# One stage of a four-layer network: the instruction orders of three engines laid out anew, other PSUM banks, three weight loads, factors in fours

## The chip, the cores and the metric

The program runs on one core of a Trainium2 chip. A core has TensorE (PE in the profile; its weight loads are PEld), VectorE (DVE), ScalarE (ACT), GpSimd (POOL) and SyncE (SP, which here only issues DMAs). Each engine works through its own list of instructions in order and waits at semaphores for the others. TensorE writes to PSUM, a memory of 8 banks of 2 KB per partition. The metric is the device time of one execution in microseconds (us).

## The reference

The network has four layers of cross-attention and feed-forward on x, (2, 1024, 256). The change touches the feed-forward of layer 1, whose two weights are reduced to three values times one scale (the code calls it the one-bit stage):

```python
def act_quant(x):
    scale = 127.0 / jnp.clip(jnp.max(jnp.abs(x), axis=-1, keepdims=True), 1e-05)
    return jnp.clip(jnp.round(x * scale), -128, 127) / scale

h = bit_linear(x, w1)                        # 256 -> 1024, on act_quant(x)
h = depthwise_conv1d(h.transpose(0, 2, 1), conv_w, conv_b)   # 3 taps along the tokens
h = jax.nn.silu(h.transpose(0, 2, 1))
return bit_linear(h, w2)                     # 1024 -> 256, on act_quant(h)
...
x = x + jnp.tanh(g_ffn[1]) * _L1_ffn_ref(_layernorm(x, axis=-1), L1_ffn_w1, ...)
# two steps later, the ternary layer, of whose weights the mean magnitude is needed first:
alpha = jnp.mean(jnp.abs(w))
w_t = jnp.sign(w) * (jnp.abs(w) > 0.5 * alpha)
```

## The kernel before

The 2048 tokens are 16 tiles of 128; tiles 0 to 7 are batch 0 (b = 0), 8 to 15 batch 1. x stays in SBUF as `K.x`. The stage is the class `BitFfn`, object `bit`; its steps are called one by one from hand-written lists, one per engine, at the end of `expert_choice_ffn`. Nothing else sets the order: an instruction starts when its engine has finished the one before and its semaphores are reached.

- Input side, in units u of two tiles: ScalarE `rows` normalises, VectorE `largest(g)` finds the row maxima of four tiles, ScalarE `quantise(g)` rounds, GpSimd `multiply_back(g)` scales back into `K.room`, TensorE `turn_rows(u)` transposes into bank 4+u (u below 4) or 6 or 7, ScalarE `high_part(u)` and VectorE `low_part(u)` split the value in two.
- Hidden side, n = 0 to 15 (eight blocks f of 128 hidden features for b = 0, then for b = 1): TensorE `up(n)`, 8 matmuls of 512 columns into the bank pair `PAIR[n]`; ScalarE `centre(n)`, the middle tap and bias; VectorE `taps(n)`, the two outer taps, two instructions over 1023 elements that read the same pair; ScalarE `silu(n)`. `centre(n)` also waits for `silu(n-2)`, and `up` into a used pair waits for the `taps` that read it.
- Output side, for the eight token tiles i of each batch: TensorE `turn(b, i)` transposes the tile's 1024 hidden values into the pair `TURN[b][i]`; VectorE `scale` takes the row maximum, clips, inverts, and multiplies out a fourth value that only `residual` needs; ScalarE `scaled` rounds; TensorE `turn_back` transposes into pair 0; ScalarE `copy_back`; TensorE `down` makes 256 columns in bank 6 or 7; VectorE `residual` adds them to x and takes the row statistics.
- Beside it stands work of the layers after: `TernaryWeights` (object `tw`) loads the two weights of layer 2 (1 MB each) over `K.room`, whose tiles `turn_rows` has read by then, both after `turn_rows(7)`; VectorE sums their magnitudes in eight `sum_piece` steps, adds them in `sum_end`, TensorE makes the total, VectorE makes `limits` and `signs`. `side.first_moments`, `first_rows`, `first_turns`, `first_copies` and `first_scores` begin the next attention. A barrier of all engines closes the stage.

`turn(0, 0)` waits for `silu(7)`, so from there TensorE mixes `up` of batch 1 with the three steps of the tokens of batch 0.

Of the kernel before, what the change touches and what calls it, by code (L numbers as in the profile page):

```python
# [1934 lines left out]
class BitFfn:  # L1935
# [245 lines left out]
    def scale(self, dve, b, i):  # L2181
        n, tv = b * TB + i, self.tv
        dve.wait_ge(self.t_ps, n + 1)
        t = Steps(self.t_step, 3 * n)
# [72 lines left out]
def expert_choice_ffn(nc, ctx, K, tag, ahead, buf, layer, acc_dram, nxt, make_bit, make_side, next_weights, old, cleared):  # L2257
# [12 lines left out]
    with ExitStack() as c:  # L2270
# [33 lines left out]
        with nc.Block(no_gpsimd_drain=True) as block:  # L2304
            @block.sync
            def _(sp):
# [1183 lines left out]
```

## Time and profile before

| | us |
|---|---|
| median of 3 runs (1058.43 to 1058.56) | 1058.54 |
| the profiled execution's own time | 1058.06 |
| its span (first to last instruction) | 1056.3 |
| busy over the span: PE, DVE, ACT, POOL | 968.4, 604.9, 488.6, 287.8 |

The stage lies at 461 to 572 us of the span. The page's shares are over the whole program, of which the stage is a tenth; for the stage the trace was asked for its own windows, waits and instructions in order of time. `PEclk` is the granted clock of TensorE as a share of full speed: 1.0 is 2.4 GHz and 0.5 is 1.2 GHz.

### The profile page before, as it was taken

The numbers are of one execution on the slowest core, as the hardware profiler recorded it, in microseconds if no ns is written. First come the engines' busy times: TensorE is split into PE (matmuls) and PEld (weight loads), VectorE is DVE, ScalarE is ACT, GpSimd is POOL, SyncE is SP. The second block draws the span as 40 slices with busy tenths as digits, with TensorE's granted clock in tenths as the row PEclk, the third lists the DMA queues.
The fourth block names the chain that finished last, engine by engine and source line by source line (L and its number), as shares of the span: only waits on it lengthen the run. The fifth ranks groups of instructions, "written<-read, shape, count | busy, mean of one in ns | idle before, by whom it ended". The sixth has DMA issues, their size and how long they took to land. (4 is left out here: it accounts for less than half of the span.)

```text
span 1056.3 us, 17895 instructions
## 1 busy us (share of the span) xinstructions
PE 968.4 (92%) x6340; PEld 831.4 (79%) x6341; DVE 604.9 (57%) x1265; ACT 488.6 (46%) x744; POOL 287.8 (27%) x271
## 2 busy tenths in 40 slices
PE   6999989989999999777788889999998899999997
PEld 5778868778888888455676768877786699999996
DVE  5858769942232213679798899767585622222221
ACT  3654422121111111687675587455552466656661
POOL 2000000033454532260005110610000244444442
PEclk9999999999999999988998699999999999999999
DMA  9200040035676654002000010070113322233332
GB/s 298 62 1 21 21 141 20 20 100 152 172 207 195 172 157 100 0 1 80 1 1 2 1 41 1 29 298 21 40 42 128 118 50 45 45 50 50 50 44 32
DMA packets 62483, 79.37 MB, mean 75 GB/s; under 512 B 7324, under 2 KB 46839, under 8 KB 62423
## 3 DMA queue, kind: packets, MB, share of 16 engines
q1 hardware_dynamic: 48791, 59.95, 16.9%
q0 software_dynamic: 13632, 18.62, 10.3%
q8 instruction: 37, 0.61, 0.2%
q14 instruction: 23, 0.19, 0.1%
HBM read 60.73 MB, written 17.83 MB: 74 GB/s over the span
## 5 line engine op out<-in xcount | busy, mean ns | idle before, releaser
L3123 PEld LDWEIGHTS ps<-room,xn_sb 128*128 128x128 f32 x1248 | 145.6, 192 | 2.7 <-issue 0.8
L3123 PE MATMUL ps<-room,xn_sb 128*128 128x128 f32 x1248 | 146.3, 275 | 0.6 <-issue 0.6
L282 POOL TENSOR_TENSOR norm_vec<-norm_vec,powers 128x4 f32<-128x4 f32 (+2 forms) x27 | 29.0, 1073 | 363.4 <-DVE norm_vec L276 363.4
L3076 POOL DMA_INDIRECT out_x<-f_yo,f_give x39 | 62.0, 1590 | 109.9 <-DVE f_yo L3321 94.4
L3192 ACT ACTIVATE xn_sb<-w_L_ffn_w 128x1024 f32 x78 | 82.2, 1057 | 20.8 <-DVE f_te L3289 10.8
L3315 DVE TENSOR_TENSOR room<-room,ps 128x512 f32<-128x512 f32 x39 | 26.8, 687 | 109.5 <-PE ps L3123 109.5
L2429 PE MATMUL ps<-b_room,room 128*128 128x256 f32 x384 | 85.6, 380 | 3.7 <-DVE room L2819 1.6
L2819 DVE TENSOR_TENSOR room<-room,ps 128x1024 f32<-128x1024 f32 x24 | 29.3, 1220 | 104.0 <-issue 89.5
L2429 PEld LDWEIGHTS ps<-b_room,room 128*128 128x128 f32 x384 | 72.6, 190 | 14.1 <-issue 1.8
L2386 POOL DMA_INDIRECT acc_rows<-f_eo,f_idx x32 | 52.4, 1637 | 94.6 <-DVE f_eo L2845 50.3
L2635 ACT ACTIVATE room<-ps 128x1024 f32<-128x1024 f32 x24 | 24.6, 1024 | 115.9 <-PE ps L2409 115.9
L492 PE MATMUL ps<-a_vblk,a_pT 128*128 128x51 f32 (+1 forms) x640 | 74.8, 272 | 0.0
L3131 PE MATMUL ps<-w_L_ffn_w,room 128*128 x312 | 73.9, 380 | 0.9 <-DVE room L3315 0.9
L492 PEld LDWEIGHTS ps<-a_vblk,a_pT 128*128 128x128 f32 (+1 forms) x640 | 74.0, 192 | 0.2 <-issue 0.2
L2409 PE MATMUL ps<-f_x_room,b_room 128*128 128x256 f32 x256 | 58.7, 382 | 3.6 <-ACT f_x_room L2665 3.6
L3131 PEld LDWEIGHTS ps<-w_L_ffn_w,room 128*128 128x128 f32 x312 | 56.2, 190 | 7.1 <-issue 1.1
L736 DVE TENSOR_REDUCE a_mx<-ps 128x16 f32<-128x1232 f32 x32 | 46.0, 1437 | 27.6 <-PE ps L466 14.2
L3197 ACT ACTIVATE room<-ps 128x512 f32<-128x512 f32 x39 | 23.3, 597 | 77.9 <-PE ps L3123 77.9
L2420 PE MATMUL ps<-f_x_room,b_room 128*128 128x256 f32 x256 | 57.9, 379 | 0.0
L2409 PEld LDWEIGHTS ps<-f_x_room,b_room 128*128 128x128 f32 x256 | 48.0, 190 | 11.7 <-issue 3.8
L481 PE MATMUL ps<-ident,a_pr 128*128 128x128 f32 x320 | 47.1, 278 | 7.3 <-ACT a_pT L684 2.5
L2420 PEld LDWEIGHTS ps<-f_x_room,b_room 128*128 128x128 f32 x256 | 48.6, 190 | 6.6
(402 smaller groups left out, 2059.5 us busy)
## 6 DMA issues: line engine op xcount, KB each, us to landing
w_L_ffn_w<-in_L_ffn_w SPq DMA_DIRECT2D x24, 512.0 KB, 8.7
b_room<-in_L_ffn_Wg SPq DMA_DIRECT2D x16, 512.0 KB, 4.8
b_room<-in_L_ffn_Wu SPq DMA_DIRECT2D x16, 512.0 KB, 5.8
b_room<-in_L_ffn_Wd SPq DMA_DIRECT2D x16, 512.0 KB, 6.4
xn_rows<-xn_sb SPq DMA_DIRECT2D x8, 512.0 KB, 2.9
x_sb<-in_x SPq DMA_DIRECT2D x4, 512.0 KB, 6.1
xn_sb<-in_L_ffn_w SPq DMA_DIRECT2D x2, 1024.0 KB, 7.6
x_sb<-acc_rows SPq DMA_DIRECT2D x4, 512.0 KB, 5.4
```

What stands on the lines that cost most here:

```text
L481: m = pe.transpose(ps[0:w, 4 + r % 2, (part - lo) * P:(part - lo + 1) * P], pr[:, n % 2, part * P:part * P + w], K.ident[:, :])
L492: m = pe.matmul(ps[:, 6, h * HV:(h + 3) * HV], pT[0:w, n % 2, part, :], vblk[0:w, n // TB, part, :, :].rearrange("p j c -> p (j c)"), star ...
L736: dve.tensor_reduce(mxt, sc, AX.X, ALU.max).then_inc(sh_step, 1)
L2386: pool.indirect_dma_start(acc_dram[:, :], bass.IndirectOffsetOnAxis(ap=idx[:, n:n + 1], axis=0), eo[e % 2][:, b, :], None, compute_op=ALU. ...
L2409: m = pe.matmul(ps[:, f // 2, (f % 2) * W:(f % 2 + 1) * W], g[:, k, f * P:(f + 1) * P], rhs[k], start=(k == 0), stop=(k == KT - 1))
L2420: m = pe.matmul(ps[:, 2 + f // 2, (f % 2) * W:(f % 2 + 1) * W], u[:, k, f * P:(f + 1) * P], rhs[k], start=(k == 0), stop=(k == KT - 1))
L2429: m = pe.matmul(ps[:, 4 + p, j * D:(j + 1) * D], hT[p][:, f, j * P:(j + 1) * P], w[:, f, :], start=(f == 0), stop=(f == FT - 1))
L2819: dve.tensor_tensor(hT[p][:, :, :].rearrange("p a c -> p (a c)"), ge[p][:, :], ps[:, 2:4, :].rearrange("p a c -> p (a c)"), ALU.mult).then ...
L3076: pool.indirect_dma_start(out_rows[:, :], bass.IndirectOffsetOnAxis(ap=give[:, j:j + 1], axis=0), yo[j % 2][:, :], None, compute_op=ALU.ad ...
L3123: m = pe.matmul(ps[:, banks[p], f * P:(f + 1) * P], wb[p][:, n, i, f * P:(f + 1) * P], xsT[p][:, i * P:(i + 1) * P], start=(i == 0), stop= ...
L3131: m = pe.matmul(ps[:, Y_BANK, 0:D], hid[p][:, f * P:(f + 1) * P], w2[:, e, f, :], start=(f == 0), stop=(f == FT - 1))
L3192: act.activation(wb[p][:, n, :, :], w[:, e, :, :], ACT.Copy).then_inc(w_sb, 1)
```

## The change

It does five things, all in this stage.

1. The load of the next weights is cut in three: the first weight in two halves of 512 KB, issued after `turn_rows(1)` and `turn_rows(3)` (each half overwrites four tiles of `K.room`), the second weight after `turn_rows(7)` as before.
2. `sum_piece` waits for the half that it reads, with two more semaphores. Its four calls for the first weight stand ahead of `taps(0)` on VectorE.
3. `scale` no longer makes the fourth value; `out_factors(g)` makes it for four tiles at once, and `residual` waits for that.
4. Other bank pairs: pair 3 (banks 6 and 7) is used by `up(8)`, `up(11)` and `up(14)`, and `turn(0, 0)` and `turn(0, 7)` go to pair 2.
5. The three hand-written lists are in another order.

```diff
-    def sync(self, sp):
-        for dst, src in self.loads:
-            sp.dma_start(dst, src).then_inc(self.loaded, 16)
+    def load_up(self, sp, half):
+        dst, src = self.loads[0]
+        sp.dma_start(dst[:, half, :], src[:, half, :]).then_inc((self.half0, self.half1)[half], 16)
+
+    def load_down(self, sp):
+        dst, src = self.loads[1]
+        sp.dma_start(dst, src).then_inc(self.loaded, 16)
...
-        dve.wait_ge(self.loaded, 32)
+        dve.wait_ge((self.half0, self.half1)[q // 2] if n == 0 else self.loaded, 16)
...
-    PAIR = (0, 1, 2, 0, 1, 2, 0, 1, 2, 0, 2, 2, 2, 2, 2, 2)
-    TURN = ((1, 1, 1, 1, 1, 1, 1, 1), (1, 2, 1, 2, 1, 2, 1, 2))
+    PAIR = (0, 1, 2, 0, 1, 2, 0, 1, 3, 0, 2, 3, 2, 2, 3, 1)
+    TURN = ((2, 1, 1, 1, 1, 1, 1, 2), (1, 2, 1, 2, 1, 2, 1, 2))
...
         dve.reciprocal(tv[:, 2, n:n + 1], tv[:, 1, n:n + 1]).then_inc(self.sc_ready, 1)
-        t.did(dve.tensor_scalar(tv[:, 3, n:n + 1], tv[:, 1, n:n + 1], self.wv[:, 3, 1:2], None, ALU.mult))
+
+    def out_factors(self, dve, g):
+        n, tv = 4 * g, self.tv
+        dve.wait_ge(self.t_step, 2 * n + 8)
+        dve.tensor_scalar(tv[:, 3, n:n + 4], tv[:, 1, n:n + 4], self.wv[:, 3, 1:2], None, ALU.mult).then_inc(self.factor, 1)
...
+                sp.wait_ge(bit.x_ps, 2)
+                next_weights.load_up(sp, 0)
+                sp.wait_ge(bit.x_ps, 4)
+                next_weights.load_up(sp, 1)
                 sp.wait_ge(bit.x_ps, TB)
-                next_weights.sync(sp)
+                next_weights.load_down(sp)
...
+                bit.turn(pe, 0, 0)
+                bit.turn(pe, 0, 1, (bit.y_sb, 8))
+                bit.up(pe, 10, (bit.qf_sb, 1))
...
+                bit.up(pe, 14, (bit.x_done, 4))
+                bit.up(pe, 15, (bit.qf_sb, 7))
...
+                side.first_copies(act)
                 bit.copy_back(act, 1, 7)
-                side.first_copies(act)
```

VectorE, the start of the stage. Before (`low_part` 0 to 3, `taps(0)`, `largest(3)`; `f_va` is the buffer of the convolution):

```order
L2105 TENSOR_TENSOR f_xl_1<-ps,f_xh_1 128x2x256 [waits f3_xh_sb] x4
L2140 SCALAR_TENSOR_TENSOR f_va<-ps,f_cws,f_va 128x1023 [waits f3_y0]
L2143 SCALAR_TENSOR_TENSOR f_va<-ps,f_cws,f_va 128x1023 [waits f3_tap]
L2065 TENSOR_REDUCE f_vec<-xn_sb 128x4 [waits f3_n_by_act]
L2067 TENSOR_SCALAR f_vec<-f_vec 128x4 [waits f3_amax]
L2069 RECIPROCAL f_vec<-f_vec 128x4 [waits f3_amax]
```

Now (L974 is `sum_piece`; the two semaphores of the halves bear older names here):

```order
L2109 TENSOR_TENSOR f_xl_1<-ps,f_xh_1 128x2x256 [waits f3_xh_sb] x4
L2069 TENSOR_REDUCE f_vec<-xn_sb 128x4 [waits f3_n_by_act]
L2071 TENSOR_SCALAR f_vec<-f_vec 128x4 [waits f3_amax]
L2073 RECIPROCAL f_vec<-f_vec 128x4 [waits f3_amax]
L974 TENSOR_REDUCE tw_part<-room 128x8 [waits a0_vblk] x2
L974 TENSOR_REDUCE tw_part<-room 128x8 [waits a0_bvb] x2
L2144 SCALAR_TENSOR_TENSOR f_va<-ps,f_cws,f_va 128x1023 [waits f3_y0]
L2147 SCALAR_TENSOR_TENSOR f_va<-ps,f_cws,f_va 128x1023 [waits f3_tap]
L2109 TENSOR_TENSOR f_xl_1<-ps,f_xh_1 128x2x256 [waits f3_xh_sb] x2
```

`largest(3)` and four `sum_piece` came ahead of `taps(0)`, and `low_part` 4 and 5 directly behind it.

VectorE where the tokens of batch 0 begin, after `taps(8)`. Before (`scale(0, 0)` in four instructions, then `taps(9)`):

```order
L2185 TENSOR_REDUCE f_tv<-ps 128x1 [waits f3_t_ps]
L2187 TENSOR_SCALAR f_tv<-f_tv 128x1 [waits f3_t_step]
L2189 RECIPROCAL f_tv<-f_tv 128x1 [waits f3_t_step]
L2190 TENSOR_SCALAR f_tv<-f_tv,f_wv 128x1
L2140 SCALAR_TENSOR_TENSOR f_va<-ps,f_cws,f_va 128x1023 [waits f3_y0]
L2143 SCALAR_TENSOR_TENSOR f_va<-ps,f_cws,f_va 128x1023 [waits f3_tap]
```

Now:

```order
L2189 TENSOR_REDUCE f_tv<-ps 128x1 [waits f3_t_ps]
L2191 TENSOR_SCALAR f_tv<-f_tv 128x1 [waits f3_t_step]
L2193 RECIPROCAL f_tv<-f_tv 128x1 [waits f3_t_step]
L2189 TENSOR_REDUCE f_tv<-ps 128x1 [waits f3_t_ps]
L2191 TENSOR_SCALAR f_tv<-f_tv 128x1 [waits f3_t_step]
L2193 RECIPROCAL f_tv<-f_tv 128x1 [waits f3_t_step]
L974 TENSOR_REDUCE tw_part<-room 128x8 [waits a0_kt]
L2144 SCALAR_TENSOR_TENSOR f_va<-ps,f_cws,f_va 128x1023 [waits f3_y0]
L2147 SCALAR_TENSOR_TENSOR f_va<-ps,f_cws,f_va 128x1023 [waits f3_tap]
```

Two tokens' `scale` of three instructions each and the first piece of the second weight now stand ahead of `taps(9)`.

ScalarE at the same place. Before (`centre(10)`, `scaled(0, 0)`, `copy_back(0, 0)`, `silu(9)`, `centre(11)`, `scaled(0, 1)`):

```order
L2133 ACTIVATE f_va<-ps,w_L_ffn_conv_b,f_cws 128x1024 [waits f3_a_sb,f3_h_ps]
L2197 ACTIVATE xn_sb<-ps,f_magic,f_tv 128x1024 [waits f3_sc]
L2205 ACTIVATE f_qT<-ps,f_magic 128x1024 [waits f3_u_ps]
L2148 ACTIVATE xnT_sb<-f_va 128x1024 [waits f3_y_sb]
L2133 ACTIVATE f_va<-ps,w_L_ffn_conv_b,f_cws 128x1024 [waits f3_a_sb,f3_h_ps]
L2197 ACTIVATE xn_sb<-ps,f_magic,f_tv 128x1024 [waits f3_sc]
```

Now (`silu(8)`, `scaled(0, 0)` and `(0, 1)`, `centre(10)`, `silu(9)`, `copy_back(0, 0)`, `centre(11)`):

```order
L2152 ACTIVATE xnT_sb<-f_va 128x1024 [waits f3_y_sb]
L2205 ACTIVATE xn_sb<-ps,f_magic,f_tv 128x1024 [waits f3_sc] x2
L2137 ACTIVATE f_va<-ps,w_L_ffn_conv_b,f_cws 128x1024 [waits f3_a_sb,f3_h_ps]
L2152 ACTIVATE xnT_sb<-f_va 128x1024 [waits f3_y_sb]
L2213 ACTIVATE f_qT<-ps,f_magic 128x1024 [waits f3_u_ps]
L2137 ACTIVATE f_va<-ps,w_L_ffn_conv_b,f_cws 128x1024 [waits f3_a_sb,f3_h_ps]
```

`scaled` of both first tokens went ahead of `centre(10)`, and `copy_back(0, 0)` behind `silu(9)`.

## Rows read from the trace of the kernel before

**Rows 1.** Windows of the stage and the stretch after; busy us (instructions) per engine.
```profile
core 0: us, PE busy (x) PEld busy (x) DVE busy (x) ACT busy (x) POOL busy (x), PEclk, DMA share, GB/s
462.45:500.00 37.55, 29.07 (x111) 21.86 (x109) 30.51 (x32) 30.04 (x34) 7.34 (x7) 0.85 0.16 56
500.00:548.00 48.00, 38.52 (x264) 31.29 (x264) 41.29 (x76) 32.27 (x31) 0.00 (x0) 0.96 0.00 1
572.00:593.00 21.00, 18.31 (x73) 15.66 (x73) 14.18 (x49) 10.80 (x21) 8.35 (x6) 0.52 0.00 1
```

**Rows 2.** Waits from 462.45 to 570.45; total us, times, longest.
```profile
DVE f_va L2140 <- ACT f_va L2133: 11.6, 7, 4.0
DVE f_tv L2185 <- PE ps L2158: 0.5, 2, 0.2
ACT f_va L2133 <- PE ps L2124: 10.8, 7, 2.9
ACT xn_sb L2197 <- DVE f_tv L2189: 6.4, 7, 1.9
```

**Rows 3.** VectorE in order of time (start us, duration us): first and last steps.
```profile
459.97 2.48 DVE L2105 TENSOR_TENSOR f_xl<-ps,f_xh 128x512 fp32r<-128x512 f32 x4
466.43 1.28 DVE L2140 SCALAR_TENSOR_TENSOR f_va<-ps,f_cws,f_va 128x1023 f32<-128x1023 f32 x1 [3.98 <-ACT f_va L2133]
...
570.02 0.43 DVE L2220 BATCH_NORM_STATS2 bn_st<-x_sb 128x6 f32<-128x256 f32 x1
```

**Rows 4.** VectorE in order of time: the spacing of its steps.
```profile
495.77 1.23 DVE L2185 TENSOR_REDUCE f_tv<-ps 128x1 f32<-128x1024 f32 x1 [0.24 <-PE ps L2158]
...
497.30 0.19 DVE L2190 TENSOR_SCALAR f_tv<-f_tv,f_wv 128x1 f32<-128x1 f32 x1
497.41 1.27 DVE L2140 SCALAR_TENSOR_TENSOR f_va<-ps,f_cws,f_va 128x1023 f32<-128x1023 f32 x1
...
499.92 1.27 DVE L2140 SCALAR_TENSOR_TENSOR f_va<-ps,f_cws,f_va 128x1023 f32<-128x1023 f32 x1
...
530.10 0.68 DVE L970 TENSOR_REDUCE tw_part<-room 128x8 f32<-128x512 f32 x1
530.70 0.47 DVE L2217 SCALAR_TENSOR_TENSOR x_sb<-ps,f_tv,x_sb 128x256 f32<-128x256 f32 x1
```

**Rows 5.** ScalarE in order of time, before and after `centre(0)`.
```profile
462.02 2.06 ACT L307 ACTIVATE xn_sb<-x_sb,norm_vec  x4
...
468.02 1.21 ACT L2133 ACTIVATE f_va<-ps,w_L_ffn_conv_b,f_cws 128x1024 f32<-128x1024 f32 x1 [1.62 <-PE ps L2124]
469.24 1.28 ACT L2148 ACT_TABLE_LOAD   x1
470.53 1.06 ACT L2148 ACTIVATE b_room<-f_va 128x1024 f32<-128x1024 f32 x1
```

**Rows 6.** TensorE in order of time: `up`, transposes, and idle time before them.
```profile
461.40 0.77 PE L2124 MATMUL ps<-f_xh,f_q 128*128 128x512 f32 x1 [2.33 <-DVE f_xl L2105]
...
464.95 0.63 PE L2124 MATMUL ps<-f_xh,f_q 128*128 128x512 f32 x1
...
477.82 0.79 PE L2124 MATMUL ps<-f_xh,f_q 128*128 128x512 f32 x1 [2.60 <-DVE f_va L2143]
...
500.15 1.07 PE L2167 MATMUL ps<-ident,xn_sb 128*128 128x128 f32 x8 [2.45 <-ACT xn_sb L2197]
501.05 1.66 PE L2158 MATMUL ps<-ident,b_room 128*128 128x128 f32 x8
...
516.08 0.50 PE L2124 MATMUL ps<-f_xh,f_q 128*128 128x512 f32 x1 [1.59 <-DVE f_va L2143]
...
517.81 0.39 PE L2124 MATMUL ps<-f_xl,f_q 128*128 128x512 f32 x1
...
569.30 1.91 PE L938 MATMUL ps<-keys_a,xnT_sb 128*128 128x77 f32 x16
```

**Rows 7.** DMA issues in the stage: KB each, us to landing.
```profile
room<-in_L_ffn_w_up SPq DMA_DIRECT2D x1, 1024.0 KB, 4.9
```

**Rows 8.** GpSimd in order of time: the next attention's rows.
```profile
554.06 9.86 POOL L906 TENSOR_SCALAR xn_sb<-x_sb,norm_vec 128x256 f32<-128x256 f32 x8
```

More of the change, by code:

```diff
@@ L2556, in _ @@
                 bit.up(pe, 1, (nxt.s_x, 8))
-                bit.turn_rows(pe, 4, (bit.xl_sb, 3))
-                bit.turn_rows(pe, 5, (bit.xl_sb, 4))
+                bit.turn_rows(pe, 4)
+                bit.turn_rows(pe, 5)
                 bit.up(pe, 2)
+                bit.turn_rows(pe, 6, (bit.xl_sb, 5))
                 bit.up(pe, 3, (bit.y_sb, 1))
@@ L2562, in _ @@
                 bit.up(pe, 5, (bit.y_sb, 3))
+                bit.turn_rows(pe, 7, (bit.xl_sb, 6))
                 bit.up(pe, 6, (bit.y_sb, 4))
-                bit.turn_rows(pe, 6, (bit.xl_sb, 5))
-                bit.turn_rows(pe, 7, (bit.xl_sb, 6))
                 bit.up(pe, 7, (bit.y_sb, 5))
-                bit.up(pe, 8, (bit.y_sb, 6))
+                bit.up(pe, 8, (bit.xl_sb, 8))
                 bit.up(pe, 9, (bit.y_sb, 7))
-                bit.turn(pe, 0, 0, (bit.y_sb, 8))
-                bit.up(pe, 10, (bit.y_sb, 9))
+                bit.turn(pe, 0, 0)
@@ L2571, in _ @@
+                bit.turn(pe, 0, 1, (bit.y_sb, 8))
+                bit.up(pe, 10, (bit.qf_sb, 1))
+                bit.up(pe, 11, (bit.y_sb, 9))
                 bit.turn_back(pe, 0, 0, (bit.y_sb, 10))
-                bit.turn(pe, 0, 1, (bit.qf_sb, 1))
-                bit.up(pe, 11, (bit.y_sb, 11))
-                bit.down(pe, 0, 0, (bit.xl_sb, 7))
                 bit.turn(pe, 0, 2, (bit.qf_sb, 2))
                 bit.turn_back(pe, 0, 1, (bit.u_sb, 1))
-                bit.up(pe, 12, (bit.y_sb, 12))
@@ L2578, in _ @@
-                bit.down(pe, 0, 1, (bit.xl_sb, 8))
+                bit.up(pe, 12, (bit.y_sb, 11))
                 bit.turn(pe, 0, 3, (bit.qf_sb, 3))
                 bit.turn_back(pe, 0, 2, (bit.u_sb, 2))
+                bit.down(pe, 0, 0, (bit.y_sb, 12))
+                bit.down(pe, 0, 1)
+                bit.turn(pe, 0, 4, (bit.qf_sb, 4))
                 bit.up(pe, 13, (bit.y_sb, 13))
                 bit.turn_back(pe, 0, 3, (bit.u_sb, 3))
+                bit.turn(pe, 0, 5, (bit.qf_sb, 5))
@@ L2591, in _ @@
+                bit.up(pe, 15, (bit.qf_sb, 7))
                 bit.turn_back(pe, 0, 5, (bit.u_sb, 5))
-                bit.down(pe, 0, 4, (bit.x_done, 3))
-                bit.turn(pe, 0, 7, (bit.qf_sb, 7))
+                bit.down(pe, 0, 4, (bit.y_sb, 15))
+                bit.turn(pe, 0, 7)
                 bit.turn_back(pe, 0, 6, (bit.u_sb, 6))
-                bit.down(pe, 0, 5, (bit.x_done, 4))
+                bit.turn(pe, 1, 0, (bit.y_sb, 16))
+                bit.down(pe, 0, 5)
+                bit.turn(pe, 1, 1, (bit.qf_sb, 8))
@@ L2596, in _ @@
+                bit.turn_back(pe, 0, 7, (bit.u_sb, 7))
                 bit.down(pe, 0, 6, (bit.x_done, 5))
-                bit.turn_back(pe, 0, 7, (bit.u_sb, 7))
-                bit.turn(pe, 1, 0, (bit.qf_sb, 8))
+                bit.turn(pe, 1, 2, (bit.qf_sb, 9))
                 bit.down(pe, 0, 7, (bit.x_done, 6))
-                bit.turn(pe, 1, 1, (bit.y_sb, 16))
-                bit.turn_back(pe, 1, 0, (bit.u_sb, 8))
-                bit.turn(pe, 1, 2, (bit.qf_sb, 9))
-                bit.down(pe, 1, 0, (bit.x_done, 7))
+                bit.turn_back(pe, 1, 0)
@@ L2720, in _ @@
                 bit.silu(act, 5)
-                bit.high_part(act, 7)
                 bit.centre(act, 7)
@@ L2925, in _ @@
                 bit.low_part(dve, 3)
+                bit.largest(dve, 3)
+                bit.tw.sum_piece(dve, 0, 0)
+                bit.tw.sum_piece(dve, 0, 1)
+                bit.tw.sum_piece(dve, 0, 2)
+                bit.tw.sum_piece(dve, 0, 3)
                 bit.taps(dve, 0)
-                bit.largest(dve, 3)
+                bit.low_part(dve, 4)
+                bit.low_part(dve, 5)
                 bit.taps(dve, 1)
```

122 lines of the change are left out of this document (59 added, 63 removed).

## The prediction

> **What bounds the stage now.** I read the windows first, then the waits, then VectorE and TensorE in order of time. The page's totals (TensorE 92% busy) are a mean over the whole program and say nothing here. In the windows [rows 1] VectorE is the fullest engine of the stage: 30.51 of 37.55 us and 41.29 of 48.00, against TensorE's 29.07 and 38.52, part of which ran below full clock (0.85 and 0.96). The waits [rows 2] show where VectorE's idle time comes from: 11.6 us in 7 waits of `taps` for `centre`, 0.5 us for a transpose. `centre` in turn waited 10.8 us for `up`, and `scaled` 6.4 us for `scale`. So this is a ring of three engines in which none is full, and what ends last is the order in which they serve each other. The longest wait is the first, 3.98 us ahead of `taps(0)` [rows 3].
>
> VectorE's own account: from the end of `low_part(3)` (459.97 + 2.48 = 462.45) to its last instruction (570.02 + 0.43 = 570.45) are 108.0 us [rows 3]. Idle are 11.6 + 0.5 = 12.1 [rows 2], so the work with its gaps is 95.9. TensorE ends 0.8 us later, at 569.30 + 1.91 = 571.2 [rows 6], and the barrier follows. The stage can gain at most the 12.1 us of idle and what is taken off the work.
>
> **The edits with a price of their own.**
> - Factors in fours. The fourth instruction of `scale` takes 497.41 - 497.30 = 0.11 us of VectorE [rows 4]. Sixteen go, four of 128x4 come: 12 x 0.11 = 1.3 us less. The new wait of `residual` is for an instruction that stands ahead of it on the same engine; its bound is one fresh wait of 0.1 us per group, so between 0.9 and 1.3. I take 1.3.
> - Three loads. SP waits for `turn_rows(1)` and `(3)` with nothing else queued behind but the second weight. The fourth `turn_rows` is over before the 461.40 of `up(0)` [rows 6]; a load of 1024 KB landed in 4.9 us [rows 7], so the second half, 512 KB, is there by 466.3 at the latest. Its readers come after 467 (below). Price 0; if a load were later than that, every us would count, since VectorE would stand before `taps(0)`.
> - Banks. No instruction is added. The new pairs only lift or add waits, which the walk below contains.
>
> **The new order, walked through.** I take the three new lists, the semaphores in the code, and spacings of the trace: `scale` 1.64 less 0.11 = 1.53, `taps` 499.92 - 497.41 = 2.51, `sum_piece` 0.60 [rows 4], four rows of ScalarE 2.06, `centre` 1.2 [rows 5], `up` (464.95 - 461.40) 3.5 us at half clock and (517.81 - 516.08) x 8/7 = 2.0 at full, eight transposes 1.0 [rows 6].
> - Start. ScalarE ends `rows(3)` at 462.02 + 2.06 = 464.1 [rows 5]. VectorE idles until then (1.65 us), does `largest(3)` to 465.7 and four `sum_piece` (2.4 us) to 468.1. ScalarE quantises to 467.8 and ends `centre(0)` at 469.0. So `taps(0)` starts at 469.0, which is 2.6 later than before, but `largest(3)` and half of the sums are behind it. Idle here: 1.65 + 0.9, instead of 3.98.
> - `taps(0)` to `taps(8)`. Each `up` comes out at least 1.5 us ahead of its `centre`, and each `centre` just as VectorE is free. The `low_part` steps that before stood between fall in the same gaps. I get `taps(8)` at 491.6 and no wait over 0.1.
> - Tokens of batch 0. With `turn(0, 0)` in pair 2 and `turn(0, 1)` in pair 1, two `scale` stand together (494.1 to 497.2) while ScalarE rounds the first. `up(10)` waits for that rounding, until 497.0; `taps(10)` then starts at 500.3, `taps(12)` at 509.2, where VectorE has waited 0.6 for `turn(0, 3)`. From there `scale`, `residual` and the pieces of the second weight fill the pauses; `taps(15)` starts at 527.0, the last `residual` of batch 0 ends at 538.0, with about 0.5 us of further waits.
> - Batch 1. `first_moments` comes near 544 instead of 551, so that GpSimd's eight rows, 9.86 us [rows 8], end some 3 us before the stage does. VectorE has 22 us of work left and TensorE 17.6 (20 groups of eight at 0.88) plus `first_scores`; I find no wait over 0.2. `down(1, 7)` now waits for a `copy_back` behind `first_copies` and starts at 557.8, and `first_scores` ends at 560.7.
>
> New account of VectorE: work 95.9 - 1.3 = 94.6, idle 1.65 + 0.9 + 1.1 = 3.65, end at 462.45 + 98.25 = 560.7, 9.8 us earlier. TensorE's end moves from 571.2 to 560.7, 10.5. I take 10.0.
>
> **What I take off.** The walk is full of ties (a result that arrives within 0.2 us of its use); I allow 0.5 us. The clock: TensorE fell to 1.2 GHz with idle stretches of 2.60 and 2.45 us, and not with 1.59 [rows 6]. The walk has one pause of 2.3 us (before `up(10)`), and several of 1.5 to 1.8. One fall costs an `up` 1.5 us. I charge two thirds of one, 1.0. The gain is 10.0 - 0.5 - 1.0 = 8.5.
>
> The silu table load took 1.28 us and the `silu` began 0.01 us behind it [rows 5]. The Trainium skill, "ScalarE: Activation LUTs", What ACT_TABLE_LOAD costs, adds a drain and gives about 2.66 us for the pair; by that the second `centre` after it would be 1.4 us later and, after the 0.6 us of slack that the walk has there, the gain 0.7 us smaller. The trace differs, and I go by it.
>
> **Rivals.**
> - A, small gain. The ties fail: each of the about 30 handoffs from `scale` to `scaled` to `turn_back` to `copy_back` runs late by 0.1 to 0.15 us, since the spacings were measured with other neighbours. Half of the 8.5 us that idle time gave (12.1 - 3.65) comes back: gain 4.3 + 1.3 less 1.0 for the clock = 4.6, time 1053.5. For it: 6.4 us of such waits before [rows 2]. Against: VectorE's durations hardly vary. Chance 0.18.
> - B, the clock in the next stage. After the barrier TensorE ran at 0.52 for 21 us, with 18.31 us busy [rows 1]. Its tail before the barrier is denser now than it was. If it starts that stretch at full clock, its 18.3 busy us shrink to about 10, of which perhaps half is on the path: 4 to 5 us more, time 1045. Against: the pause of the barrier itself stays. Chance 0.12.
> - C, no change. The halves land late or a wait that I overlooked holds `taps(0)` and one later chain; this needs a stall of 8 us or a lasting spread of small ones. Nothing in the rows has it. 1056.5 to 1060.5, chance 0.04.
> - D, slower. TensorE in batch 0's tokens, 493 to 538, at 1.2 GHz. There it has 6 `up` and 27 groups of eight: at full 6 x 1.9 + 27 x 0.88 = 35 of 45 us; at half, with about 1.5 per group (one took 1.66 with its tail [rows 6]) and 3.5 per `up`, 61.5. With a share h at half it needs 35 + 26.5h. It delays anything from h = 0.38, and eats the whole 10 us from h = 0.76; all of it at half gives 16 us, less 10 gained: 1064. For it: many pauses between small groups. Against: 0.96 over 500 to 548 [rows 1], or h = 0.08, with longer pauses. Chance 0.04. This is what the Trainium skill, "TensorE: Matmul & The Clock Gate", A second HAM failure mode: psum-queue depth-cycling, warns of (short idle times between groups that cycle through banks make the clock swing); by that rule the time would lie between A and D. The trace agrees only for the early stretch, 0.85 before 500 us [rows 1], where `up` has slack.
>
> **How the numbers follow.** Against its own time: 1058.06 - 8.5 = 1049.6; the median of the runs is 0.5 above the profiled execution, so I give 1049.8. The forecast's own range is 1047.5 to 1052.5, chance 0.62; below it lies B, above it A, then C and D. For 8 in 10 I take half of B and most of A: 1045.8 to 1054.5. Under 0.2% (2.1 us) a change of this kernel can't be told from none. Faster 0.92 (forecast, A, B), same 0.04, slower 0.04.
>
> **What would show it.** In the trace after: `taps(0)` starts near 469.0 with four `sum_piece` ahead of it and no wait for a load; the waits of `taps` for `centre` shrink from 11.6 to below 3 us; two `scale` stand together before `taps(9)`; VectorE is over 95% busy from 469 to its end, which comes near 561 to 562; the stage after starts 8 to 10 us earlier and takes as long as before. I am wrong on A if those waits stay above 5 us, on D if the granted clock from 493 to 538 is under 0.8, and on the load if VectorE waits for SP before `taps(0)`. The stages before 455 should not move at all.

## The result and the profile after

| | before | after |
|---|---|---|
| median of the runs, us | 1058.55 (1058.43 to 1058.80, 4 runs) | 1050.82 (1049.33 to 1051.95, 4 runs) |
| ratio, 95% interval | | 0.9933 [0.9909, 0.9957] |
| the profiled execution's own time, us | 1058.06 | 1049.91 |
| its span, us | 1056.3 | 1048.2 |

The change makes the kernel 7.7 us faster (0.7%). 1049.8 was forecast, with 1045.8 to 1054.5 as the range. The changed kernel's line numbers are 4 to 8 higher than those of before (`taps` L2144, `scale` L2189, `up` L2128).

First the windows of the changed kernel, the same two stretches as in [rows 1], and the 20 us that follow its barrier.

```profile
core 0: us, PE busy (x) PEld busy (x) DVE busy (x) ACT busy (x) POOL busy (x), PEclk, DMA share, GB/s
462.45:500.00 37.55, 28.56 (x119) 21.40 (x119) 34.64 (x38) 30.47 (x34) 6.74 (x6) 0.91 0.09 28
500.00:548.00 48.00, 42.34 (x320) 36.24 (x319) 44.25 (x83) 38.11 (x36) 1.67 (x2) 0.99 0.00 1
563.90:583.90 20.00, 17.21 (x72) 14.87 (x72) 14.04 (x48) 10.58 (x21) 8.35 (x6) 0.57 0.00 1
```

In the first stretch VectorE is busy 34.64 us instead of 30.51, in the second 44.25 instead of 41.29. Then VectorE's waits over the stage, to be laid beside [rows 2].

```profile
DVE f_va L2144 <- ACT f_va L2137: 2.0, 2, 1.1
DVE f_vec L2069 <- ACT xn_sb L307: 1.7, 1, 1.7
DVE f_tv L2189 <- PE ps L2162: 1.1, 2, 0.8
```

The seven waits of `taps` for `centre`, 11.6 us, have become two of 2.0 us together. New is one of `largest(3)` for the rows that ScalarE still makes. Where they stand is seen in VectorE's instructions in order of time (start, duration, in brackets the idle time before it and what ended it); they answer to [rows 3].

```profile
459.37 2.48 DVE L2109 TENSOR_TENSOR f_xl<-ps,f_xh 128x512 fp32r<-128x512 f32 x4
463.51 1.22 DVE L2069 TENSOR_REDUCE f_vec<-xn_sb 128x4 f32<-128x1024 f32 x1 [1.67 <-ACT xn_sb L307]
...
465.06 2.43 DVE L974 TENSOR_REDUCE tw_part<-room 128x8 f32<-128x512 f32 x4
468.39 1.28 DVE L2144 SCALAR_TENSOR_TENSOR f_va<-ps,f_cws,f_va 128x1023 f32<-128x1023 f32 x1 [0.89 <-ACT f_va L2137]
...
490.88 1.28 DVE L2144 SCALAR_TENSOR_TENSOR f_va<-ps,f_cws,f_va 128x1023 f32<-128x1023 f32 x1
...
500.71 1.28 DVE L2144 SCALAR_TENSOR_TENSOR f_va<-ps,f_cws,f_va 128x1023 f32<-128x1023 f32 x1 [1.11 <-ACT f_va L2137]
...
561.13 0.43 DVE L2228 BATCH_NORM_STATS2 bn_st<-x_sb 128x6 f32<-128x256 f32 x1
```

The first row starts 0.6 us earlier than before. That isn't the change: in the second trace of the same kernel (after again, below) it starts at 459.97, as before. So I measure the stage from here on by itself: from the start of `low_part(0)` (this first row) to TensorE's first instruction behind the barrier. That was 572.82 - 459.97 = 112.85 us before and is 563.89 - 459.37 = 104.52 now: the stage gained 8.3 us. TensorE around `up(10)` and at the barrier, in order of time:

```profile
496.29 0.50 PE L2128 MATMUL ps<-f_xh,f_q 128*128 128x512 f32 x1 [2.21 <-ACT xn_sb L2205]
...
497.10 0.63 PE L2128 MATMUL ps<-f_xl,f_q 128*128 128x512 f32 x1
497.52 0.63 PE L2128 MATMUL ps<-f_xh,f_q 128*128 128x512 f32 x1
...
560.03 1.91 PE L938 MATMUL ps<-keys_a,xnT_sb 128*128 128x77 f32 x16
563.89 0.63 PE L1061 MATMUL ps<-ident,xn_sb 128*128 128x128 f32 x4 [1.96 <-PEq L100]
```

The clock did fall at `up(10)`: its matmuls follow each other every 0.42 us, where they take 0.23 at full clock.

### The profile page after: what moved, and what is told of

It is laid out like the page before. It is cut to its first block and busy times, and to the rows that moved or that the text cites. A ratio compares the mean times of both kernels' runs of the same rounds, so it can differ in the third digit from the quotient of the medians.

```text
span 1048.2 us, 17878 instructions
## 1 busy us (share of the span) xinstructions
PE 964.9 (92%) x6340; PEld 829.7 (79%) x6341; DVE 603.3 (58%) x1253; ACT 489.6 (47%) x744; POOL 288.2 (27%) x271
## 5 line engine op out<-in xcount | busy, mean ns | idle before, releaser
L2398 POOL DMA_INDIRECT acc_rows<-f_eo,f_idx x32 | 52.4, 1638 | 94.6 <-DVE f_eo L2857 49.6
```

The costliest lines, as they stand in the source:

```text
L2398: pool.indirect_dma_start(acc_dram[:, :], bass.IndirectOffsetOnAxis(ap=idx[:, n:n + 1], axis=0), eo[e % 2][:, b, :], None, compute_op=ALU. ...
```

## Experiments

"After" is the changed kernel. Each ratio is to runs of the kernel before on the same chip. Most executions of one kernel lie within 4 to 5 us of each other, single ones further off (of 59 executions of the kernel before that ran beside these experiments 56 took 1055.1 to 1059.7 us, and one 1064.0). So the stage's length in the trace, as defined above, is the finer measure, but each length is from one trace.

| kernel | ratio, 95% interval | stage, us | against `after` |
|---|---|---|---|
| before | | 112.85 | +8.3 |
| after | 0.9933 [0.9909, 0.9957] | 104.52 | |
| after again | 0.9932 [0.9914, 0.9950] | 104.53 | 0.0 |
| fours_only (on before) | 1.0010 [0.9997, 1.0023] | 112.76 | -0.1 against before |
| sums_only (on before) | 1.0004 [0.9981, 1.0026] | 112.90 | 0.0 against before |
| start_new_tokens_old | 1.0000 [0.9986, 1.0014] | 111.34 | -1.5 against before |
| fours_undone | 0.9938 [0.9918, 0.9958] | 104.59 | +0.1 |
| sums_late | 0.9969 [0.9953, 0.9984] | 108.10 | +3.6 |
| banks_old | 1.0136 [1.0118, 1.0155] | 126.50 | +22.0 |
| ups_old | 1.0104 [1.0081, 1.0128] | 118.04 | +13.5 |
| fill | 0.9916 [0.9898, 0.9935] | 102.92 | -1.6 |
| start | 0.9932 [0.9907, 0.9957] | 102.14 | -2.4 |
| best | 0.9906 [0.9891, 0.9921] | 101.99 | -2.5 |
| best_hold | 0.9901 [0.9870, 0.9931] | 102.02 | -2.5 |

**after again**, the changed kernel once more, without an edit.

> The changed kernel itself, once more, for its spread: its four runs so far lie in two pairs, 1049.3 and 1049.9, and 1051.7 and 1052.0, while the kernel before keeps within 0.4 us. Theory: the stage ends at the same time in each (first TensorE row after the barrier at 563.9, within 0.4), and the 2 us come later, from how long TensorE stays at 1.2 GHz in the stages after. Rival: they come from inside the stage, from the fall of the clock at up(10); then VectorE's wait for centre(10) varies between 0 and 1.2 us and the barrier with it. Time 1049.3 to 1052 in both.

The stage took 104.53 us, the kernel 1049.11 (1048.05 to 1051.55). In these two traces the stage repeats to 0.01 us, and what differs lies behind it (2.5 us, the last section) and ahead of it (0.6 us). It isn't always as close. Where the lists are the same up to `taps(8)`, that step starts 31.5 us behind the start of the stage in five traces (after, after again, fours_undone, banks_old and fill) and 32.4 in ups_old, whose granted clock was 0.50 from 472.8 to 479.6, where theirs was 1.00. I read differences of the stage below 1 us as open, unless VectorE's rows explain them.

**sums_late**, the four sums of the first weight back among the tokens:

```diff
-                bit.tw.sum_piece(dve, 0, 0)   # and 1, 2, 3, ahead of taps(0)
...
                 bit.out_factors(dve, 0)
+                bit.tw.sum_piece(dve, 0, 0)
+                bit.tw.sum_piece(dve, 0, 1)
...
                 bit.scale(dve, 0, 5)
+                bit.tw.sum_piece(dve, 0, 2)
...
+                bit.tw.sum_piece(dve, 0, 3)
                 bit.scale(dve, 0, 6)
```

> The changed kernel with the four magnitude sums of the first weight put back among the tokens of batch 0 (two behind scale(0, 3), one each behind scale(0, 5) and ahead of scale(0, 6)); loads, banks, factors and all other orders stay. Theory (VectorE's work after taps(0) sets the end): taps(0) still starts at 468.4, since ScalarE's quantise(3) stands ahead of centre(0), with 3.3 us of idle ahead of it instead of 0.9, and the 2.4 us of sums are paid later: 1050.8 + 2.4 = 1053.2, less at most 0.5 that fits into waits. Rival (the ring of handoffs sets the end, VectorE has room): the sums fall into pauses and the time stays within 0.7 of 1050.8.

The stage is 3.6 us longer. VectorE and TensorE in order of time:

```profile
469.24 1.28 DVE L2144 SCALAR_TENSOR_TENSOR f_va<-ps,f_cws,f_va 128x1023 f32<-128x1023 f32 x1 [3.24 <-ACT f_va L2137]
...
520.30 1.23 DVE L2189 TENSOR_REDUCE f_tv<-ps 128x1 f32<-128x1024 f32 x1 [1.73 <-PE ps L2162]
```
```profile
514.81 0.50 PE L2128 MATMUL ps<-f_xh,f_q 128*128 128x512 f32 x1 [1.23 <-DVE f_va L2147]
...
515.88 0.63 PE L2128 MATMUL ps<-f_xl,f_q 128*128 128x512 f32 x1
```

The wait ahead of `taps(0)` is 3.24 us instead of 0.89: the 2.35 us that the sums had filled are idle again, as the theory had it. The rest goes with another fall of the clock, at `up(12)`, after a pause of only 1.23 us, and 1.73 us of wait behind it.

**fours_only and sums_only**, one part each on the kernel before: the factors in fours, and the two half loads with the four sums ahead of `taps(0)`.

```diff
-        t.did(dve.tensor_scalar(tv[:, 3, n:n + 1], tv[:, 1, n:n + 1], self.wv[:, 3, 1:2], None, ALU.mult))
+    def out_factors(self, dve, g): ...        # fours_only, behind scale(b, 3) and scale(b, 7)
```
```diff
+                bit.tw.sum_piece(dve, 0, 0)   # sums_only; also 1, 2, 3; none of them later
                 bit.taps(dve, 0)
```

> The kernel before with the out factors made four at a time (12 instructions of VectorE fewer, 1.3 us of its work), nothing else changed. Theory (before the change the ring of three engines sets the pace in batch 0 and VectorE's work only in batch 1): about half of it counts, 0.5 to 0.9 us faster: 1057.7 to 1058.0. Rival (VectorE's work counts all through): 1.3 us, 1057.2. Rival (nothing): 1058.5.

> The kernel before with the loads in three pieces and the four magnitude sums of the first weight ahead of taps(0), where VectorE idled 3.98 us; all else as before. Theory: the 2.4 us of sums cost nothing in the new place; in the old places about half of them lay in VectorE's pauses in batch 0, so 1 to 1.8 us are gained: 1056.7 to 1057.5. Rival (all counts): 2.4 us, 1056.1. Rival (the old pauses hid them): within 0.4 us of before.

Neither moves the stage (112.76 and 112.90), so in both the rival holds by which nothing is gained. In sums_only the wait of `taps(0)` shrinks from 3.98 to 1.61 us, but VectorE's waits for `centre` sum to nearly what they were (11.6 before):

```profile
DVE f_va L2144 <- ACT f_va L2137: 11.1, 7, 2.5
```

In fours_only they sum to 10.6, and those for a transpose to 1.9 instead of 0.5. In the old order VectorE's work isn't what sets the end; time taken off it comes back as waiting.

**start_new_tokens_old**, the kernel before with the new loads and the new lists up to `taps(8)`, and the old lists and banks from there:

```diff
                 bit.taps(dve, 8)              # up to here as in the changed kernel
                 bit.scale(dve, 0, 0)          # from here as before
                 bit.taps(dve, 9)
```

> Half of the change: loads in three, and the new orders of all three engines up to taps(8), up(7) and silu(8); from scale(0, 0), up(8) and centre(10) on the old orders and old banks, and the factors one by one. Theory (VectorE's account): at taps(8) it is 1.3 us earlier than before, as the changed kernel is (491.5 against 492.9 with equal starts), and the 2.4 us of sums are behind it; then the old ring with its waits of about 8 us takes over and swallows part of the 2.4: gain 2 to 3.7 us, 1054.9 to 1056.5. The other 4 to 6 us belong to the token part. Rival (the gain is made at the start): 6 us or more are gained here.

The stage is 1.5 us shorter, of 8.3, and less than the 2 to 3.7 expected; the ratio of whole kernels, 1.0000 with an interval of 0.14% to either side, can't tell it from nothing. Of its waits for `centre` 7.7 us in 5 are left, three of them (2.20, 2.26 and 1.41 us) at `taps(11)` to `taps(13)`. Most of the gain is in the token part, where the new lists and the new banks come together.

**fours_undone**, the changed kernel with the fourth instruction back in each `scale`:

```diff
+        t.did(dve.tensor_scalar(tv[:, 3, n:n + 1], tv[:, 1, n:n + 1], self.wv[:, 3, 1:2], None, ALU.mult))
-                bit.out_factors(dve, 0)       # and 1, 2, 3
```

> The changed kernel with the factors made one by one as before; all else stays. Theory (VectorE is now the bound from taps(0) to the end): all 12 extra instructions count, 1.2 us slower than the changed kernel, 1052.0 against 1050.8. Rival (they fit in waits): within 0.5 us of it.

The stage is 0.1 us longer, and VectorE's last instruction 0.25 us later (102.00 instead of 101.75 us from the start). Two pieces of VectorE's time order, first after again, then fours_undone, tell why:

```profile
546.57 0.17 DVE L276 TENSOR_SCALAR norm_vec<-norm_vec 128x8 f32<-128x8 f32 x1
546.65 0.22 DVE L2198 TENSOR_SCALAR f_tv<-f_tv,f_wv 128x4 f32<-128x4 f32 x1
546.98 0.48 DVE L2225 SCALAR_TENSOR_TENSOR x_sb<-ps,f_tv,x_sb 128x256 f32<-128x256 f32 x1
```
```profile
546.23 0.20 DVE L2194 TENSOR_SCALAR f_tv<-f_tv,f_wv 128x1 f32<-128x1 f32 x1
546.35 0.17 DVE L267 TENSOR_TENSOR norm_vec<-bn_st 128x8 f32<-128x8 f32 x1
```

A fourth instruction costs 0.12 us to the next start. `out_factors` costs 0.33 where `residual` waits for it at once (two of the four stand so) and 0.12 to 0.15 elsewhere. From `scale(1, 1)` to the end of VectorE that is 7 x 0.12 - 0.33 - 0.15 = 0.36 us saved, and the traces differ by 0.34 there; the like saving ahead of it is hidden, since the waits for `centre` and `turn` are 3.1 us with the fours and 2.7 without. The rival (they fit in waits) holds.

**banks_old**, the three new orders with the old bank pairs and the waits that they need:

```diff
-    PAIR = (0, 1, 2, 0, 1, 2, 0, 1, 3, 0, 2, 3, 2, 2, 3, 1)
-    TURN = ((2, 1, 1, 1, 1, 1, 1, 2), (1, 2, 1, 2, 1, 2, 1, 2))
+    PAIR = (0, 1, 2, 0, 1, 2, 0, 1, 2, 0, 2, 2, 2, 2, 2, 2)
+    TURN = ((1, 1, 1, 1, 1, 1, 1, 1), (1, 2, 1, 2, 1, 2, 1, 2))
...
-                bit.turn(pe, 0, 1, (bit.y_sb, 8))
-                bit.up(pe, 10, (bit.qf_sb, 1))
-                bit.up(pe, 11, (bit.y_sb, 9))
+                bit.turn(pe, 0, 1, (bit.qf_sb, 1))
+                bit.up(pe, 10, (bit.y_sb, 9))
+                bit.up(pe, 11, (bit.y_sb, 11))
```

> The changed kernel with the bank pairs of the kernel before (up(8) in pair 2, up(11) and up(14) in pair 2, up(15) in pair 2, turn(0, 0) and turn(0, 7) in pair 1) and the waits that go with them; the three orders stay new. Theory (orders and banks belong together): turn(0, 1) now waits for the rounding of the first token, so scale(0, 1), which stands ahead of taps(9), comes about 3 us later, and up(11) to up(15) each wait for the taps that read pair 2, so that taps(11) waits about 3 us for centre(11) and taps(14), taps(15) 2 to 3 us each: the stage is 6 to 12 us longer than the 104.5 of the changed kernel, that is as long as before (112.9) or longer. Rival (the orders carry the gain, banks only remove small waits): stage 105 to 107.5.

The stage takes 126.5 us, 13.7 more than before, beyond both expectations. VectorE's long waits in it:

```profile
499.25 1.23 DVE L2189 TENSOR_REDUCE f_tv<-ps 128x1 f32<-128x1024 f32 x1 [3.29 <-PE ps L2162]
513.03 1.23 DVE L2189 TENSOR_REDUCE f_tv<-ps 128x1 f32<-128x1024 f32 x1 [6.56 <-PE ps L2162]
520.23 1.23 DVE L2189 TENSOR_REDUCE f_tv<-ps 128x1 f32<-128x1024 f32 x1 [3.09 <-PE ps L2162]
541.67 1.28 DVE L2144 SCALAR_TENSOR_TENSOR f_va<-ps,f_cws,f_va 128x1023 f32<-128x1023 f32 x1 [5.11 <-ACT f_va L2137]
549.38 1.28 DVE L2144 SCALAR_TENSOR_TENSOR f_va<-ps,f_cws,f_va 128x1023 f32<-128x1023 f32 x1 [4.52 <-ACT f_va L2137]
```

They sum to 22.6 us, about the whole loss of 22.0. The granted clock from 500 to 548 us is 0.78 in this kernel. The new orders without the new banks are far worse than the old orders. The opposite kernel, the old orders with the new banks, was not run; what the banks are worth by themselves is not shown.

**ups_old**, only `up(11)` and `up(14)` back in pair 2:

```diff
-    PAIR = (0, 1, 2, 0, 1, 2, 0, 1, 3, 0, 2, 3, 2, 2, 3, 1)
+    PAIR = (0, 1, 2, 0, 1, 2, 0, 1, 3, 0, 2, 2, 2, 2, 2, 1)
...
-                bit.up(pe, 11, (bit.y_sb, 9))
+                bit.up(pe, 11, (bit.y_sb, 11))
-                bit.up(pe, 14, (bit.x_done, 4))
+                bit.up(pe, 14, (bit.y_sb, 14))
```

> The changed kernel with up(11) and up(14) alone back in pair 2, where they wait for the taps of the block before that read the same pair; turn(0, 0), turn(0, 7) and up(8) keep their new pairs. With all banks old the stage took 126.5 us, 22 more than the 104.5 of the changed kernel, and VectorE's long waits were 3.3 us ahead of scale(0, 1), 6.6 and 3.1 ahead of scale(0, 2) and (0, 3), 5.1 and 4.5 ahead of taps(14) and (15). Theory (what counts is that up(11) and up(14) can run ahead of the taps of up(10) and up(13)): four of those five waits come back, and the stage is 12 to 18 us longer than 104.5. Rival (the first token's pair is what sets the rest going, the ups only follow): the waits ahead of scale(0, 2) and (0, 3) shrink below 3 us in sum and the stage is 4 to 8 us longer.

The stage is 13.5 us longer than in the changed kernel, in the theory's range. 0.9 of them stand ahead of `taps(8)`, where nothing was edited (see after again), so about 12.6 belong to the two pairs. Three waits return, not four (VectorE, and then the `up(11)` that causes the first one, on TensorE):

```profile
511.11 1.22 DVE L2189 TENSOR_REDUCE f_tv<-ps 128x1 f32<-128x1024 f32 x1 [6.67 <-PE ps L2162]
518.31 1.22 DVE L2189 TENSOR_REDUCE f_tv<-ps 128x1 f32<-128x1024 f32 x1 [3.09 <-PE ps L2162]
539.42 1.28 DVE L2144 SCALAR_TENSOR_TENSOR f_va<-ps,f_cws,f_va 128x1023 f32<-128x1023 f32 x1 [4.78 <-ACT f_va L2137]
```
```profile
504.49 0.80 PE L2128 MATMUL ps<-f_xh,f_q 128*128 128x512 f32 x1 [3.93 <-DVE f_va L2147]
```

`turn(0, 2)` stands behind `up(11)` on TensorE, so when `up(11)` waits 3.93 us for `taps(10)` to free its pair, and then runs at half clock, the next `scale` waits too. The price holds the falls of the clock that the new waits bring with them; the trace doesn't separate the two.

**fill**, 16 transposes of the identity into banks that nothing reads, ahead of `up(10)`:

```diff
                 bit.turn(pe, 0, 1, (bit.y_sb, 8))
+                pe.wait_ge(bit.y_sb, 9)
+                bit.keep_busy(pe, 16)
                 bit.up(pe, 10, (bit.qf_sb, 1))
```

> The changed kernel with 16 transposes of the identity (into banks 6 and 7, which nobody reads then) between turn(0, 1) and up(10), where TensorE idled 2.21 us and then ran at 1.2 GHz for 3.4 us. They end before the wait of up(10) does. Theory (the fall of the clock costs what VectorE then waits): up(10) takes 1.9 instead of 3.2 us, VectorE's wait of 1.11 us for centre(10) goes to below 0.2, and 0.8 to 1.3 us of the time go, if the next wait, for turn(0, 3), does not take them. Rival (the ring has slack behind up(10)): within 0.3 us of the changed kernel.

**start**, `centre(0)` ahead of `quantise(3)` on ScalarE, two sums ahead of `largest(3)` on VectorE:

```diff
-                bit.quantise(act, 3)
                 bit.centre(act, 0)
+                bit.quantise(act, 3)
...
-                bit.largest(dve, 3)
                 bit.tw.sum_piece(dve, 0, 0)
                 bit.tw.sum_piece(dve, 0, 1)
+                bit.largest(dve, 3)
```

> The changed kernel with centre(0) ahead of quantise(3) on ScalarE (it idled 1.71 us there, waiting for largest(3)) and two of the four sums ahead of largest(3) on VectorE (it idled 1.67 us there). Theory (all of VectorE's idle ahead of taps(0) is on the path): taps(0) starts at 466.3 to 466.6 instead of 468.4, and about 2 us of the time go. Rival (quantise(3), pushed by centre(0), delays turn_rows(6) and with it up(3), or centre(1) comes late): taps(0) is early and taps(1) or taps(2) wait for it; under 0.7 us are gained.

The five us after the start of `up(10)`, windows of after, of fill and of start:

```profile
496.29:501.29 5.00, 5.00 (x15) 3.97 (x16) 3.82 (x6) 3.02 (x3) 0.00 (x0) 0.66 0.01 3
```
```profile
496.95:501.95 5.00, 5.00 (x28) 4.29 (x29) 4.81 (x7) 3.62 (x4) 0.00 (x0) 1.00 0.00 0
```
```profile
496.66:501.66 5.00, 5.00 (x28) 4.30 (x29) 4.82 (x7) 3.62 (x4) 0.00 (x0) 1.00 0.00 0
```

In fill the pause before `up(10)` is 0.47 us, the clock stays at 2.4 GHz, `taps(10)` doesn't wait, and the stage is 1.6 us shorter, the price of that fall and more than the 0.8 to 1.3 expected. That the transposes are what kept the clock up isn't shown by this one trace. In start the clock stays up as well, though nothing was done for it and the pause is as long as in after:

```profile
496.66 0.50 PE L2128 MATMUL ps<-f_xh,f_q 128*128 128x512 f32 x1 [2.22 <-ACT xn_sb L2205]
```

So of its 2.4 us 1.6 are the fall that didn't happen, and about 0.8 the order: `taps(8)` starts 30.7 us behind `low_part(0)` instead of 31.5. `taps(0)` even starts at 6.9 instead of 9.0, as expected, but of these 2.1 us 1.07 are waited for again at `taps(2)`. The whole kernel, 1048.48 us with a ratio of 0.9932, can't be told from the changed one.

**best**, start and fill together.

> The changed kernel with both improvements that the earlier runs pointed to: centre(0) ahead of quantise(3) on ScalarE and two sums ahead of largest(3) on VectorE, and 16 transposes of the identity on TensorE ahead of up(10), so that the clock doesn't fall there. Alone they shortened the stage by 2.4 and 1.6 us (104.5 to 102.1 and to 102.9). If they are independent the stage takes 100.5 to 101.0 us and the kernel 1046.5 to 1047.5 where the kernel before takes 1056.5. Rival: in the better start up(10) no longer has a pause long enough for the clock to fall, so the transposes have nothing to save, and the stage stays at 102.0 to 102.3.

The stage took 101.99 us, the kernel 1048.10 (1045.36 to 1048.65): the rival's number, and not by its reason. The rival said that the pause would be too short; it was there in start, 2.22 us. What was missing was the fall, and so the transposes had nothing to save. It beats the kernel before by 0.94%, and in the stage the changed kernel by 2.5 us; the two ratios (0.9906 and 0.9933) have intervals that overlap.

**best_hold**, best with 12 more transposes in the stage behind the barrier, for rival B:

```diff
                 turn_a(2)
+                for j in range(12):
+                    pe.transpose(ps[:, 5, (j % 4) * P:(j % 4 + 1) * P], K.ident[:, :], K.ident[:, :])
                 turn_p(0)
```

> As best, and in the stage after the barrier 12 more transposes of the identity into a bank that is free there, between the first four transposes and those that wait 1.42 us for ScalarE's softmax. Question: whether that stretch, which ran 20 us at 1.2 GHz in all kernels so far, is held at 2.4 GHz when the second of its two pauses (1.95 us at the barrier, 1.42 us right behind) is filled. If it is: TensorE's busy 17 to 18 us of the 20 shrink by half, and the kernel is 3 to 5 us faster than best (rival B of the prediction). If the pause of the barrier alone makes the clock fall: nothing, or up to 1 us slower, since the 12 transposes take 1.3 us at full and 2.6 at half clock.

The first 20 us behind the barrier, best and then best_hold; and TensorE in order of time in best_hold:

```profile
561.83:581.83 20.00, 17.37 (x72) 15.01 (x72) 14.04 (x48) 10.54 (x21) 8.31 (x6) 0.57 0.01 1
```
```profile
562.55:582.55 20.00, 15.39 (x95) 13.40 (x96) 16.67 (x55) 12.55 (x23) 8.34 (x6) 0.91 0.01 1
```
```profile
565.95 1.99 PE L1105 MATMUL ps<-ctx_nat,f_pT 77*128 77x256 f32 x8 [0.25 <-ACT f_pT L1264]
570.17 2.82 PE L938 MATMUL ps<-keys_a,xnT_sb 128*128 128x77 f32 x16 [2.23 <-ACT xnT_sb L1253]
```

The clock was held, 0.91 instead of 0.57; in the 13 other traces the same 20 us stand at 0.50 to 0.57, so here the transposes are the cause. From the barrier to the first row of the stage after that one are 106.92 us instead of 109.51: 2.6 us. TensorE then waits 2.23 us for ScalarE; the stretch was bound by more than TensorE. The kernel as a whole took 1048.23 us (1043.26 to 1053.51), the same as best, where 3 to 5 us less were expected: in the profiled execution the program behind that point took 377.5 us instead of 372.3. In it the clock fell for 3.4 us behind that point and again 24 us later, and for 10.2 us at 800 us, where best has one stretch of 3.4. Whether the transposes bring this about, or it is the spread of the last section, one trace doesn't tell.

## Why the prediction was right, and where its terms were off

The walk, counted from the start of `low_part(0)` (459.97 in the prediction, 459.37 in after):

| step | predicted | measured |
|---|---|---|
| `taps(0)` starts | 9.0 | 9.0 |
| `taps(8)` starts | 31.6 | 31.5 |
| `up(10)` starts, pause | 37.0, 2.3 | 36.9, 2.2 |
| `taps(10)` starts | 40.3 | 41.3 |
| wait of `scale(0, 3)` | 0.6 | 0.8 |
| `taps(15)` starts | 67.0 | 68.7 |
| last `residual` of batch 0 ends | 78.0 | 79.9 |
| `first_moments` | 84.0 | 85.8 |
| VectorE ends | 100.7 | 102.2 |
| gain of the stage | 10.0 - 1.5 = 8.5 | 8.3 |

- **What bounds the stage.** Right: the order in which the engines serve each other. VectorE's idle time for `centre` went from 11.6 to 2.0 us. It is 94.4% busy from `taps(0)` to its end (87.97 of 93.17 us); over 95% was forecast.
- **Where the gain comes from.** Right as a whole, and the experiments add what the walk couldn't show: fours, sums and the new start bring nothing, nothing and 1.5 us in the old token part, and the orders without the banks lose 13.7 us against before. The prediction had given the banks no price of their own and left them to the walk. They are the largest condition of the change that was measured: `up(11)` and `up(14)` in pair 3 alone are worth about 12.6 us in this order. How the remaining 6.8 us of gain split between the lists of the three engines is open; none of the lists was put back alone in the token part.
- **VectorE's account.** From the end of `low_part(3)` (461.85) to its end (561.56) are 99.7 us, 4.7 of them idle and 95.0 work. The walk had 3.65 and 94.6, and 1.5 us were allowed for ties and the clock. So the account missed 1.1 us of idle and 0.4 of work, 1.5 in all. That the two match to 0.1 us is in part luck, since the clock was priced too low and the ties and the fours too high.
- **Factors in fours, 1.3 us.** Wrong in size: 0.1 us of the stage, 0.25 of VectorE's end. The 0.11 us that I had taken for the new instruction is 0.33 where its reader stands right behind it (1.0 us of work saved instead of 1.3 in all), and most of that fell into waits, which grew by 0.4 us. The lower bound of 0.9 left out that the saving could be hidden.
- **Loads at price 0.** Right. The halves were issued at 454.8 and 458.5 and landed in 3.2 us (median), and the sums began at 465.06 without a wait for them. Moving the sums early was worth 3.6 us in the new order, of which 2.35 are the filled wait.
- **The clock, 1.0 us.** The place was right, the price 1.6 (two thirds of 1.5 had been charged), and the reason was wrong. I had read from [rows 6] that pauses of 2.45 us and more make the clock fall and 1.59 doesn't. It fell behind 1.23 us in sums_late and stayed behind 2.22 in start. Behind longer pauses it stayed too: 2.82 us in banks_old and 2.93 in ups_old, with 1.00 in the five us that follow each. The 2.2 us pause of the walk was therefore neither safe nor sure to cost, and that two thirds of a fall were near the measured price is luck.
- **Ties, 0.5 us.** From `taps(10)` on the measured steps lie 1.0 to 1.9 us behind the walk, and 1.5 at the end. The fall explains 1.0 at `taps(10)` and 1.6 of the stage by fill, so about nothing is left for the ties. The gain of the stage, 8.5 by the sum and 8.3 measured, is right by 0.2 us with fours and ties too large and the clock too small.
- **The table load.** As before, `silu(0)` begins 0.01 us behind the load:

```profile
470.43 1.28 ACT L2152 ACT_TABLE_LOAD   x1
471.72 1.06 ACT L2152 ACTIVATE b_room<-f_va 128x1024 f32<-128x1024 f32 x1
```

  The 2.66 us of the Trainium skill, "ScalarE: Activation LUTs", What ACT_TABLE_LOAD costs, don't appear between the `centre` before, which ends at 470.41, and the `silu`. (The prediction's sum by that page, 1.4 less 0.6 us of slack, is 0.8 and not the 0.7 that it gives.)
- **From 8.5 us to 1049.8.** The prediction adds 0.5 us to 1049.6 and writes 1049.8; by its own terms it is 1050.1, which lies nearer to the measured 1050.8.
- **Rival A (small gain)** fails by its own mark: 2.0 us of waits for `centre`, where it needed more than 5. **Rival D (slower)** too: the granted clock from 493 to 538 us is 0.96. Its mechanism exists, though: in banks_old the clock is 0.78 over 500 to 548 us and the kernel 1.4% slower than before. **Rival B (the clock in the next stage)** didn't come by itself, 0.57 instead of 0.50 in the 20 us behind the barrier. Forced in best_hold it gave 2.6 us, less than the 4 to 5 of the prediction; TensorE's 2.23 us of wait for ScalarE there show that it no longer sets the path alone.
- **From 8.3 to 7.7 us.** The two profiled executions differ by 8.1 us: 0.6 ahead of the stage, 8.3 in it, 0.5 in the stage after it (109.46 us instead of 110.01), less 1.3 in the rest of the program (374.8 instead of 373.5). The medians of the runs differ by 7.7. The parts outside the stage aren't the change's: fours_only, whose stage is as long as before, has 109.44 and 372.25 there. The 0.6 us ahead of it, where the prediction had allowed for no movement, are gone in the second trace of the same kernel.

## What to carry over

When three engines serve each other in a ring, price a new order by walking the lists with the spacings of the trace: here the walk was within 0.1 us up to the first fall of the clock and within 2 us behind it. The price of a single part was no guide: the orders without their banks lose 13.7 us where both together gain 8.3. Ask of every order which buffers let it run ahead, and try the order without them: here a producer that was moved forward into a bank that was still read held everything queued behind it. A few cheap instructions placed in an engine's known wait are worth what they fill, but time taken off an engine that waits later comes back as waiting.

## What the runs showed of the hardware

**The same pause with and without a fall of the clock.** Behind the pause before `up(10)`, 2.21 us in after and 2.22 in start, the granted clock of the next 5 us was 0.66 and 1.00. The same holds for one kernel in two executions. At the first matmul behind the second barrier after the change, windows of after and of after again:

```profile
673.35:678.35 5.00, 5.00 (x23) 4.16 (x24) 1.38 (x9) 1.68 (x4) 1.95 (x3) 0.66 0.68 229
```
```profile
673.95:678.95 5.00, 5.00 (x30) 4.37 (x31) 1.38 (x9) 1.52 (x4) 1.94 (x3) 1.00 0.71 222
```

The idle time ahead was 2.37 and 2.36 us. A fall at this place, one some 35 us later, or both, goes with differences of 1.2 to 3.1 us between executions. From this point to the end the program took

- 372.2 to 372.4 us in after again, best, fours_undone and fours_only, where the clock stayed up over these 70 us;
- 373.5 to 373.7 in before, fill, sums_only, start_new_tokens_old and banks_old, with the second fall alone;
- 373.6 in ups_old and 374.0 in start, with the first alone;
- 374.8 in after and 375.4 in sums_late, with both.

Only best_hold, 377.5, lies outside. The Trainium skill, "TensorE: Matmul & The Clock Gate", What's actually happening, says that the gate looks at TensorE's activity on a schedule of its own which doesn't start anew with the kernel, so that the point of a change depends on where work lands in it. The rows agree in so far as neither the pause's length alone nor the kernel alone decides it; they don't show the schedule.

**A wait for one's own result.** VectorE's [128, 4] `out_factors` took 0.33 us to the next start where the next instruction waited for it (546.04 to 546.37 in after) and 0.12 where the next one was `taps` and didn't (510.00 to 510.12). Here the wait, 0.2 us, is worth more than the instruction.
